# Self attention on one core: output casts moved to ScalarE, casts ahead of the exponentials, three waits for maxima dropped

## The chip, the cores and the metric

The kernel runs on one core of a Trainium2 chip. The metric is the device time of one execution, in microseconds (us): the median of the runs shown.

## What is computed

A transformer block on x of shape (4, 1024, 256): self attention, cross attention to a context of 77 rows, and a feed-forward part, each with a residual. The change is in the self attention alone. From the reference, cut to this:

```
attn_in = _adaln(x, cond, ln1_w, ln1_b, g1_w, g1_b, b1_w, b1_b)
x = _attn(attn_in, attn_in, sa_wq, sa_wkv, sa_wo, sa_bo) + x

def _attn(xq, ctx, wq, wkv, wo, bo):        # H, DH = 16, 64
    q = _heads(xq @ wq)
    k, v = jnp.split(ctx @ wkv, 2, axis=-1)
    k = _heads(k)
    v = _heads(v)
    q = _rope(q, sq, cq)
    k = _rope(k, sk, ck)
    sim = jnp.einsum('bhnd,bhmd->bhnm', q, k) * DH ** (-0.5)
    a = jax.nn.softmax(sim, axis=-1)
    o = jnp.einsum('bhnm,bhmd->bhnd', a, v)
    ...
    return o @ wo + bo
```

## The kernel before, in words

Each engine runs its own list of instructions in the order in which the code writes it; nothing else schedules them. Engines wait for each other through semaphores (`wait_ge`).

The self attention works through 32 head pairs (G = 4 batches x 8 pairs of heads; `g` in the code, numbered 0 to 31). A pair has eight **key tiles** of 128 keys (`kt`, 0 to 7). While pair g is being attended to, pair g+1's score maxima are estimated, pair g+2's keys and pair g+3's queries are projected and rotated, and pair g-1's output is divided by its sums and split. In one tile:

- TensorE: `differences` (L451), `scores` (L474), `bases` (L458), `shift` (L481), which subtracts the estimated maxima, then `values` of the tile before in two halves (L496). Between the two halves stands, by tile, a projection (L55: keys in tiles 0 and 1, queries in 4 and 5), the second half of the values' projection (L43, tile 2), a norm's transposes (L531), the sums (L506, tile 0) or the output product. At the end of tile 7 the maxima are transposed (L651) and the next pair's values projected (L43). Ahead of what stands between the halves TensorE waits for the first half of the tile's maxima (L621, `maxima_free(j, kt, 1)`), and ahead of the next tile's `differences` for the second half. All of these use the PSUM tile `ps_t`, which is why they take turns.
- ScalarE: `rises` (L692) reads what `differences` wrote, then two `exponentials` of 128x1024 (L704). By tile also: `high` (L688), which casts a rotated key or query to its f16 high part; `evacuate_kq` (L678), which takes a projected half out of PSUM, and for which the next `differences` waits; `evacuate_v` (L683), `evacuate_o` (L711), `evacuate_sums` (L717); `row` (L696), the negated maxima as a row. In pairs with a norm: `logarithms` (L721), `inverse_roots` (L726), `normalise` (L730), `norm_affine` (L737) and `norm_high` (L742).
- VectorE: `maxima` (L869) in two halves of 128x512, then `add_probs` (L882) twice. By tile also: `multiply` (L848, L849) and `rotated` (L853, and L856 for the key differences), `low` (L861), `reciprocals` (L886), `divide` (L892), and `split_output`: the cast of the divided output to its high half (L897) and the low half as the difference (L899). In pairs with a norm: statistics (L909, L915) and `norm_low` (L957).
- SyncE's queue carries the swaps of the rotation, the row of maxima, the gathering of sums and the broadcast of their inverses.

Pairs differ: 5, 10, 16, 21 and 28 take the statistics of the next norm, the two pairs that lie 2 and 3 behind these have its transposes in tiles 3 and 6, and pairs 9, 17 and 25 have the output product of a whole batch between their tiles.

## Time and profile before

| | us |
|---|---|
| median of 3 runs | 2208.25 |
| lowest, highest | 2205.37, 2210.38 |
| profiled execution | 2206.14 |
| its span | 2204.2 |

The profile is of one execution. "Busy" is the time in which an engine had an instruction in work; matmuls overlap, and their ends are modelled. In a timeline, rows are in order of start, a bracket at the end gives the idle time before the row and what ended it, and rows of a kind are merged (x4 are four instructions). The start of a pair or a tile is here the start of its first `differences` (L451). The self attention takes the time from about 75 to 1558 us; the cross attention and the feed-forward part follow.

### The profile page before, as it was taken

The numbers are of one execution on the slowest core, as the hardware profiler recorded it, in microseconds if no ns is written. First come the engines' busy times: TensorE is split into PE (matmuls) and PEld (weight loads), VectorE is DVE, ScalarE is ACT, GpSimd is POOL, SyncE is SP. The second block draws the span as 40 slices with busy tenths as digits, with TensorE's granted clock in tenths as the row PEclk, the third lists the DMA queues.
The fourth block names the chain that finished last, engine by engine and source line by source line (L and its number), as shares of the span: only waits on it lengthen the run. The fifth ranks groups of instructions, "written<-read, shape, count | busy, mean of one in ns | idle before, by whom it ended". The sixth has DMA issues, their size and how long they took to land. (4 is left out here: it accounts for less than half of the span.)

```text
span 2204.2 us, 40751 instructions
## 1 busy us (share of the span) xinstructions
PE 2057.2 (93%) x16360; PEld 919.9 (42%) x16360; DVE 1787.5 (81%) x2793; ACT 1395.5 (63%) x1774; POOL 9.0 (0%) x10
## 2 busy tenths in 40 slices
PE   4799999999999999999999999999988999986999
PEld 2233333336333334533333453333632444454676
DVE  6789899986998999699999869987688888845654
ACT  4577767774777777577777657776367666633442
POOL 1000000000000000000000000000000000000000
PEclk8799999999999999999999999999998999987999
DMA  6010110011110101011101112111232333324111
GB/s 191 37 39 31 49 49 37 33 49 49 49 50 30 59 30 50 30 68 49 39 30 45 35 46 72 40 49 40 79 120 93 108 122 123 122 77 120 39 39 39
DMA packets 99281, 135.42 MB, mean 61 GB/s; under 512 B 34501, under 2 KB 72343, under 8 KB 99095
## 3 DMA queue, kind: packets, MB, share of 16 engines
q1 hardware_dynamic: 99095, 132.83, 18.3%
q8 instruction: 130, 2.13, 0.4%
q14 instruction: 56, 0.46, 0.1%
HBM read 67.29 MB, written 13.11 MB: 36 GB/s over the span
## 5 line engine op out<-in xcount | busy, mean ns | idle before, releaser
L704 ACT ACTIVATE sa_probs<-sa_ps_s 128x1024 f32<-128x1024 f32 x512 | 496.6, 1022 | 212.5 <-PE sa_ps_s L481 212.4
L496 PE MATMUL sa_ps_o<-sa_probs,sa_v_pair 128*64 128x512 f32 x2048 | 534.7, 611 | 11.3 <-DVE sa_mx L869 11.3
L882 DVE TENSOR_TENSOR sa_acc<-sa_acc,sa_probs 128x1024 f32<-128x1024 f32 x384 | 452.9, 1221 | 18.7 <-ACT sa_probs L704 10.8
L869 DVE CUSTOM_DVE_ANT_0 sa_rise<-sa_ps_t,sa_rise 128x512 f32<-128x512 f32 x504 | 327.2, 687 | 132.1 <-PE sa_ps_t L458 130.5
L474 PE MATMUL sa_ps_s<-scores_or_weights 64*128 64x512 f16 x3072 | 376.3, 377 | 1.2 <-ACT raw_or_keys L678 1.2
L692 ACT ACTIVATE sa_rise<-sa_ps_t 128x1024 f32<-128x1024 f32 x252 | 257.6, 1022 | 151.5 <-PE sa_ps_t L451 150.4
L474 PEld LDWEIGHTS sa_ps_s<-scores_or_weights 64*128 64x128 f16 x3072 | 155.4, 94 | 153.6 <-ACT sa_v_pair L683 6.8
L496 PEld LDWEIGHTS sa_ps_o<-sa_probs,sa_v_pair 128*64 128x64 f32 x2048 | 113.7, 135 | 164.8 <-issue 97.0
L451 PE MATMUL sa_ps_t<-sa_kd,scores_or_weights 64*128 64x512 f16 x504 | 99.6, 389 | 37.1 <-ACT raw_or_keys L678 17.6
L451 PEld LDWEIGHTS sa_ps_t<-sa_kd,scores_or_weights 64*128 64x128 f16 x504 | 26.3, 93 | 220.7 <-issue 183.2
L458 PE MATMUL sa_ps_t<-scores_or_weights 64*128 64x512 f16 x504 | 98.8, 386 | 10.4 <-ACT sa_rise L692 10.4
L481 PE MATMUL sa_ps_s<-sa_m_line,sa_m_ones 32*128 32x512 f16 x1024 | 101.2, 385 | 0.0
L882 DVE TENSOR_TENSOR sa_acc<-sa_probs 128x1024 f32<-128x1024 f32 x64 | 75.6, 1222 | 8.4 <-ACT sa_probs L704 6.0
L848 DVE TENSOR_TENSOR raw_or_keys<-raw_or_keys,ropeC 128x1024 f32<-128x1024 f32 x64 | 78.1, 1220 | 4.6 <-DMA sa_swp<-raw_or_keys 4.5
L678 ACT ACTIVATE raw_or_keys<-sa_ps_t 128x512 f32<-128x512 f32 x118 | 70.9, 601 | 15.0 <-PE sa_ps_t L55 13.9
L43 PE MATMUL ca_ps_t<-xT_hi,scores_or_weights 128*128 128x512 f16 x256 | 79.3, 392 | 0.0
L861 DVE TENSOR_TENSOR scores_or_weights<-raw_or_keys,scores_or_weights 128x1024 f16<-128x1024 f32 x62 | 75.6, 1219 | 1.7 <-ACT scores_or_weights L688 1.7
L853 DVE TENSOR_TENSOR raw_or_keys<-raw_or_keys,sa_swp 128x1024 f32<-128x1024 f32 x62 | 75.8, 1222 | 1.1
L849 DVE TENSOR_TENSOR sa_swp<-sa_swp,ropeS 128x1024 f32<-128x1024 f32 x62 | 75.6, 1219 | 0.0
L1991 ACT ACTIVATE ff_hid<-ff_ps_h,ff_b_col 128x1024 f32<-128x1024 f32 x32 | 35.6, 1114 | 61.3 <-PE ff_ps_h L43 61.3
L43 PE MATMUL ca_ps_t<-scores_or_weights,ca_o_hi 128*128 128x256 f16 x400 | 74.2, 283 | 0.0
L43 PE MATMUL ff_ps_y<-w_hi,ff_h_hi 128*128 128x256 f16 x256 | 69.8, 273 | 3.5 <-DVE ff_h_lo L2090 3.5
(322 smaller groups left out, 3636.0 us busy)
## 6 DMA issues: line engine op xcount, KB each, us to landing
sa_swp<-raw_or_keys SPq DMA_DIRECT2D x124, 256.0 KB, 2.4
sa_inv<-sa_scratch SPq DMA_DIRECT2D x128, 128.0 KB, 3.0
ca_swp<-raw_or_keys SPq DMA_DIRECT2D x64, 256.0 KB, 2.3
ca_inv<-ca_scratch SPq DMA_DIRECT2D x64, 256.0 KB, 3.9
sa_xs<-in_x SPq DMA_DIRECT2D x4, 1024.0 KB, 5.8
sa_xr<-in_x SPq DMA_DIRECT2D x4, 1024.0 KB, 7.1
x_after_cross<-scores_or_weights SPq DMA_DIRECT2D x32, 128.0 KB, 2.0
ff_xr<-x_after_cross SPq DMA_DIRECT2D x4, 1024.0 KB, 5.7
```

The lines of the kernel that those rows point to most:

```text
L43: ins = pe.matmul(out, lhs[a][lhs_at(k)], rhs[b][rhs_at(k)], start=(start and i == 0), stop=(stop and i == len(terms) - 1))
L451: ins = pe.matmul(max_banks(j, t)[:, half(x)], hi[rows(x), j % 3, 1, t * P:(t + 1) * P], kd[rows(x), j % 2, :], start=True, stop=True)
L458: ins = pe.matmul(max_banks(j, t)[:, half(x)], hi[rows(x), j % 3, 1, t * P:(t + 1) * P], hi[rows(x), j % 3, 0, 0:HALF], start=True, stop=True)
L474: pe.matmul(ps_s[c][:, half(x)], k[rows(x), s, 0, ks], q[rows(x), s, 1, half(c)], start=(n == 0), stop=False)
L481: ins = pe.matmul(ps_s[c][:, half(x)], m_ones[quarter, :], m_line[quarter, :], start=False, stop=True)
L496: ins = pe.matmul(ps_o[rows(x), half(c)], v_pair[:, kt, rows(x)], probs[:, kt % 2, c, half(x)], start=(kt == 0), stop=(kt == NK - 1))
L692: act.activation(rise_of(j, t), max_banks(j, t), ACT.Relu).then_inc(s_rise, 1)
L704: act.activation(probs[:, kt % 2, c, :], ps_s[c][:, :], ACT.Exp, scale=float(DH) ** -0.5).then_inc(s_p, 1)
L848: dve.tensor_tensor(raw[:, i, :], raw[:, i, :], ropeC[:, :], ALU.mult).then_inc(s_mul[i], 1)
L853: dve.tensor_tensor(raw[:, i, :], raw[:, i, :], swapped(j, i)[:, :], ALU.add).then_inc(s_rot[i], 1)
L869: dve.tensor_tensor_reduce(out=larger, in0=max_banks(j, t)[:, half(x)], in1=larger, scale=1.0, scalar=-3.0e38, op0=ALU.add, op1=ALU.max, a ...
L882: dve.tensor_tensor(acc[:, c, :], before, probs[:, kt % 2, c, :], ALU.add).then_inc(s_acc[c], 1)
```

## The change

It has four parts.

1. On ScalarE `high(g+2, 1)` moves from behind tile 1's exponentials to ahead of them, and `high(g+2, 0)` from behind tile 5's exponentials to ahead of tile 6's.
2. The cast to the output's high half goes from VectorE to ScalarE: `split_output` becomes `high_output` (ScalarE, ahead of the exponentials of tile 5 for half 0 and of tile 7 for half 1; both in tile 7 in pairs 9, 17 and 25) and `low_output` (VectorE).
3. VectorE's order within a pair: `reciprocals` ahead of `low` in tile 1, `divide` of half 0 in tile 4 ahead of the rotation instead of tile 5, of half 1 in tile 5 instead of 6, and the key differences on their own in tile 5.
4. TensorE's wait for the first half of the maxima is dropped in tiles where nothing stands between the two halves of `values` (3, 6 and 7, unless a norm's transpose is there).

```diff
-                    if j < G:
+                    if j < G and (kt in K_AT + Q_AT + (V_SECOND,) or norm_bank(g, kt) is not None):
                         maxima_free(j, kt, 1)
...
+            def high_output(g, c):
+                act.wait_ge(s_div, 2 * g + c + 1)
+                if g >= PAIRS and g % PAIRS == 0:
+                    act.wait_ge(s_y, TT * (g // PAIRS))
+                act.activation(o_hi[:, g % PAIRS, half(c)], o_pair[:, half(c)], ACT.Copy).then_inc(s_ohi, 1)
...
+                    if kt == 1 and g + 2 < G:
+                        high(g + 2, 1)
+                    if kt == 5 and g >= 1 and not late_norm(g):
+                        high_output(g - 1, 0)
+                    if kt == 6 and g + 2 < G:
+                        high(g + 2, 0)
+                    if kt == 7 and g >= 1:
+                        if late_norm(g):
+                            high_output(g - 1, 0)
+                        high_output(g - 1, 1)
                     if g >= 0:
                         for c in order(kt):
                             exponentials(g, kt, c)
...
-                    if kt == 1 and g + 2 < G:
-                        high(g + 2, 1)
-                    if kt == 5 and g + 2 < G:
-                        high(g + 2, 0)
...
-            for n in range(2, len(following)):
+            for n in range(2, 5):
+                following_high(n)
+            for c in range(2):
+                high_output(G - 1, c)
+            for n in range(5, len(following)):
                 following_high(n)
...
-                if i == 0:
-                    dve.wait_ge(s_rot[0], j + 1)
-                    dve.tensor_tensor(kd[:, j % 2, :], raw[:, 0, HALF:N], raw[:, 0, 0:HALF],
-                                      ALU.subtract).then_inc(s_kd, 1)
+
+            def key_differences(j):
+                dve.wait_ge(s_rot[0], j + 1)
+                dve.tensor_tensor(kd[:, j % 2, :], raw[:, 0, HALF:N], raw[:, 0, 0:HALF],
+                                  ALU.subtract).then_inc(s_kd, 1)
...
-            def split_output(g, c):
+            def low_output(g, c):
                 n, cs = 2 * g + c + 1, half(c)
-                dve.wait_ge(s_div, n)
-                dve.tensor_copy(o_hi[:, g % PAIRS, cs], o_pair[:, cs]).then_inc(s_ohi, 1)
                 dve.wait_ge(s_ohi, n)
                 dve.tensor_tensor(o_lo[:, g % PAIRS, cs], o_pair[:, cs], o_hi[:, g % PAIRS, cs],
                                   ALU.subtract).then_inc(s_ot, 1)
...
+                    if kt == 1 and g >= 1:
+                        reciprocals(g - 1)
                     if kt == 1 and g + 2 < G:
                         low(g + 2, 1)
-                    if kt == 1 and g >= 1:
-                        reciprocals(g - 1)
                     if kt == 2 and g + 2 < G:
                         multiply(g + 2, 0)
+                    if kt == 4 and g >= 1:
+                        divide(g - 1, 0)
                     if kt == 4 and g + 2 < G:
                         rotated(g + 2, 0)
...
+                    if kt == 5 and g + 2 < G:
+                        key_differences(g + 2)
+                    if kt == 5 and g >= 1 and not late_norm(g):
+                        low_output(g - 1, 0)
                     if kt == 5 and g >= 1:
-                        divide(g - 1, 0)
-                        if not late_norm(g):
-                            split_output(g - 1, 0)
-                    if kt == 6 and g >= 1:
                         divide(g - 1, 1)
-                    if kt == 6 and late_norm(g) and g + 2 < G:
-                        low(g + 2, 0)
...
-                    if kt == 7 and g + 2 < G and not late_norm(g):
+                    if kt == 7 and g + 2 < G:
                         low(g + 2, 0)
                     if kt == 7 and g >= 1:
                         if late_norm(g):
-                            split_output(g - 1, 0)
-                        split_output(g - 1, 1)
+                            low_output(g - 1, 0)
+                        low_output(g - 1, 1)
```

How it stands in the engines' lists is shown at three places of pair 15; the changed file has other line numbers, given in the words. First ScalarE in tile 1 and the start of tile 2, before (L692 is a rise, L704 the exponentials, L688 the cast of the query, L678 the evacuation of a projected key):

```order
L692 ACTIVATE sa_rise<-sa_ps_t 128x1024
L704 ACTIVATE sa_probs<-sa_ps_s 128x1024 x2
L688 ACTIVATE scores_or_weights<-raw_or_keys 128x1024
L678 ACTIVATE raw_or_keys<-sa_ps_t 128x512
L692 ACTIVATE sa_rise<-sa_ps_t 128x1024
```

and the same place after:

```order
L692 ACTIVATE sa_rise<-sa_ps_t 128x1024
L688 ACTIVATE scores_or_weights<-raw_or_keys 128x1024
L704 ACTIVATE sa_probs<-sa_ps_s 128x1024 x2
L678 ACTIVATE raw_or_keys<-sa_ps_t 128x512
L692 ACTIVATE sa_rise<-sa_ps_t 128x1024
```

The cast has passed the two exponentials and stands right behind the rise. Next ScalarE in tiles 5 and 6, before:

```order
L692 ACTIVATE sa_rise<-sa_ps_t 128x1024
L704 ACTIVATE sa_probs<-sa_ps_s 128x1024 x2
L688 ACTIVATE scores_or_weights<-raw_or_keys 128x1024
L678 ACTIVATE raw_or_keys<-sa_ps_t 128x512
L692 ACTIVATE sa_rise<-sa_ps_t 128x1024
L704 ACTIVATE sa_probs<-sa_ps_s 128x1024 x2
```

and after (L717 is now `high_output`):

```order
L692 ACTIVATE sa_rise<-sa_ps_t 128x1024
L717 ACTIVATE sa_o_hi<-sa_o_pair 128x512
L704 ACTIVATE sa_probs<-sa_ps_s 128x1024 x2
L678 ACTIVATE raw_or_keys<-sa_ps_t 128x512
L692 ACTIVATE sa_rise<-sa_ps_t 128x1024
L688 ACTIVATE scores_or_weights<-raw_or_keys 128x1024
L704 ACTIVATE sa_probs<-sa_ps_s 128x1024 x2
```

The cast of the key has left the place between exponentials and evacuation in tile 5 for tile 6, and the output cast has come into tile 5. Last VectorE from tile 4's sums (L882) to the first maxima of tile 6 (L869), before:

```order
L882 TENSOR_TENSOR sa_acc<-sa_acc,sa_probs 128x1024 x2
L853 TENSOR_TENSOR raw_or_keys<-raw_or_keys,sa_swp 128x1024
L856 TENSOR_TENSOR sa_kd<-raw_or_keys 128x512
L869 ISA sa_rise,sa_mx<-sa_ps_t,sa_rise 128x512
L869 ISA sa_mx 128x1
L869 ISA sa_rise,sa_mx<-sa_ps_t,sa_rise 128x512
L869 ISA sa_mx 128x1
L882 TENSOR_TENSOR sa_acc<-sa_acc,sa_probs 128x1024 x2
L892 TENSOR_TENSOR sa_o_pair<-sa_o_pair,sa_inv 128x512
L897 CAST sa_o_hi<-sa_o_pair 128x512
L899 TENSOR_TENSOR sa_o_lo<-sa_o_pair,sa_o_hi 128x512
L869 ISA sa_rise,sa_mx<-sa_ps_t,sa_rise 128x512
```

and after (L899 now are the sums, L909 the divide, L869 the rotation, L886 the maxima, L873 the key differences, L914 the low half):

```order
L899 TENSOR_TENSOR sa_acc<-sa_acc,sa_probs 128x1024 x2
L909 TENSOR_TENSOR sa_o_pair<-sa_o_pair,sa_inv 128x512
L869 TENSOR_TENSOR raw_or_keys<-raw_or_keys,sa_swp 128x1024
L886 ISA sa_rise,sa_mx<-sa_ps_t,sa_rise 128x512
L886 ISA sa_mx 128x1
L886 ISA sa_rise,sa_mx<-sa_ps_t,sa_rise 128x512
L886 ISA sa_mx 128x1
L899 TENSOR_TENSOR sa_acc<-sa_acc,sa_probs 128x1024 x2
L873 TENSOR_TENSOR sa_kd<-raw_or_keys 128x512
L914 TENSOR_TENSOR sa_o_lo<-sa_o_pair,sa_o_hi 128x512
L909 TENSOR_TENSOR sa_o_pair<-sa_o_pair,sa_inv 128x512
L886 ISA sa_rise,sa_mx<-sa_ps_t,sa_rise 128x512
```

The divide of half 0 now stands ahead of the rotation, the key differences behind tile 5's sums, and the cast is gone.

## Rows read from the trace of the kernel before

**Rows 1.** The page, part 1: busy time, share and instructions of each engine.

```profile
PE 2057.2 (93%) x16360; PEld 919.9 (42%) x16360; DVE 1787.5 (81%) x2793; ACT 1395.5 (63%) x1774; POOL 9.0 (0%) x10
```

**Rows 2.** Windows of pairs 15, 14, 10: length, busy per engine, TensorE's clock, DMA.

```profile
772.21:815.18 42.97, 42.16 (x331) 15.88 (x331) 39.77 (x63) 30.60 (x36) 0.00 (x0) 1.00 0.11 38
728.86:772.21 43.35, 42.35 (x332) 15.79 (x331) 40.30 (x64) 30.69 (x36) 0.00 (x0) 1.00 0.20 62
...
549.42:594.51 45.09, 43.00 (x332) 15.49 (x331) 42.23 (x81) 33.34 (x40) 0.00 (x0) 1.00 0.19 60
```

**Rows 3.** TensorE's waits, 120 to 1560 us: for whom; total, times, longest.

```profile
PE sa_ps_t L451 <- ACT raw_or_keys L678: 14.6, 36, 0.4
PE sa_ps_o L496 <- DVE sa_mx L869: 8.6, 13, 2.1
PE sa_ps_t L55 <- DVE sa_mx L869: 7.0, 25, 0.5
```

**Rows 4.** Timeline of TensorE, pair 14, ends of tiles 1 and 4: start, length.

```profile
740.40 1.03 PE L496 MATMUL sa_ps_o<-sa_probs,sa_v_pair 128*64 128x512 f32 x4
741.83 0.39 PE L451 MATMUL sa_ps_t<-sa_kd,scores_or_weights 64*128 64x512 f16 x2 [0.41 <-ACT raw_or_keys L678]
...
755.85 1.03 PE L496 MATMUL sa_ps_o<-sa_probs,sa_v_pair 128*64 128x512 f32 x4
756.81 0.39 PE L451 MATMUL sa_ps_t<-sa_kd,scores_or_weights 64*128 64x512 f16 x2
```

**Rows 5.** Timeline of ScalarE, pair 14, tile 1 and the end of tile 4.

```profile
736.47 1.02 ACT L692 ACTIVATE sa_rise<-sa_ps_t 128x1024 f32<-128x1024 f32 x1
738.32 1.94 ACT L704 ACTIVATE sa_probs<-sa_ps_s 128x1024 f32<-128x1024 f32 x2 [0.82 <-PE sa_ps_s L481]
740.14 1.06 ACT L688 ACTIVATE scores_or_weights<-raw_or_keys 128x1024 f16<-128x1024 f32 x1
741.09 0.60 ACT L678 ACTIVATE raw_or_keys<-sa_ps_t 128x512 f32<-128x512 f32 x1
...
756.05 0.60 ACT L678 ACTIVATE raw_or_keys<-sa_ps_t 128x512 f32<-128x512 f32 x1 [0.35 <-PE sa_ps_t L55]
```

**Rows 6.** Timeline of VectorE, pair 14, tile 0 and the start of tile 6.

```profile
728.89 0.68 DVE L957 TENSOR_TENSOR xT_lo<-sa_xn,xT_hi 128x512 f16<-128x512 f32 x1
...
731.70 0.68 DVE L869 CUSTOM_DVE_ANT_0 sa_rise<-sa_ps_t,sa_rise 128x512 f32<-128x512 f32 x1
...
732.91 1.22 DVE L848 TENSOR_TENSOR raw_or_keys<-raw_or_keys,ropeC 128x1024 f32<-128x1024 f32 x1
734.05 1.22 DVE L849 TENSOR_TENSOR sa_swp<-sa_swp,ropeS 128x1024 f32<-128x1024 f32 x1
735.30 1.22 DVE L853 TENSOR_TENSOR raw_or_keys<-raw_or_keys,sa_swp 128x1024 f32<-128x1024 f32 x1
...
763.17 0.43 DVE L897 CAST sa_o_hi<-sa_o_pair 128x512 f16<-128x512 f32 x1
763.63 0.69 DVE L899 TENSOR_TENSOR sa_o_lo<-sa_o_pair,sa_o_hi 128x512 f16<-128x512 f32 x1
```

**Rows 7.** Timeline of ScalarE, pair 10's tile 7 and pair 12's tile 6.

```profile
590.40 1.28 ACT L704 ACT_TABLE_LOAD   x1
...
593.62 0.25 ACT L696 ACTIVATE sa_m_rows<-sa_ps_t 16x128 f16<-16x128 f32 x1
...
677.80 0.63 ACT L742 ACTIVATE xT_hi<-sa_xn 128x512 f16<-128x512 f32 x1
678.34 1.02 ACT L692 ACTIVATE sa_rise<-sa_ps_t 128x1024 f32<-128x1024 f32 x1
```

**Rows 8.** Timelines of pair 31: VectorE in tile 4, ScalarE and TensorE around tile 5.

```profile
1543.07 2.36 DVE L882 TENSOR_TENSOR sa_acc<-sa_acc,sa_probs 128x1024 f32<-128x1024 f32 x2 [1.97 <-ACT sa_probs L704]
...
1545.61 1.94 ACT L704 ACTIVATE sa_probs<-sa_ps_s 128x1024 f32<-128x1024 f32 x2 [1.66 <-PE sa_ps_s L481]
...
1547.36 1.47 PE L474 MATMUL sa_ps_s<-scores_or_weights 64*128 64x512 f16 x12
```

More of the change, by code:

```diff
@@ L1040, in _ @@
                 rotated(0, i)
+                if i == 0:
+                    key_differences(0)
             weights_low(4)
@@ L1048, in _ @@
                 rotated(1, i)
+                if i == 0:
+                    key_differences(1)
             for n in range(2):
@@ L1118, in _ @@
                 divide(G - 1, c)
-                split_output(G - 1, c)
+                low_output(G - 1, c)
             dve.wait_ge(s_x, 16 * B)
```

## The prediction

> **What bounds the kernel now.** The views were read in this order: the page's busy shares, the windows of single head pairs, TensorE's waits, and then the timelines of the three engines around each wait. The page gives TensorE 2057.2 us of 2204.2 us, VectorE 1787.5, ScalarE 1395.5 [rows 1]. The change touches only the self attention, which runs 32 head pairs of eight key tiles (0 to 7) from about 75 to 1558 us. A pair with no extra work (pair 15) takes 42.97 us, and TensorE is busy for 42.16 of them, VectorE for 39.77, ScalarE for 30.60 [rows 2]. The granted clock there is 1.00. So TensorE bounds, and only its own waits can be won. They are short and of few kinds [rows 3]: 14.6 us in 36 waits for ScalarE's evacuation of a projected key or query (L678), 7.0 us in 25 and 8.6 us in 13 for VectorE's maxima (L869) ahead of L55 and L496. That is 30.2 us in all, 1.4% of the time, and hardly more can be won here; further waits, for the norm's evacuation and for rises, the change leaves as they are.
>
> The recorded idle time is slightly less than a wait costs. After the last value products of tile 1 (L496 at 740.40) the next tile's L451 starts at 741.83, 1.43 us later; after those of tile 4 (755.85) it starts at 756.81, 0.96 us later and without a wait [rows 4]. So such a wait costs **0.47 us**, where the trace calls 0.41 idle.
>
> The Trainium skill ("Perfetto Trace Analysis", Identifying the Most-Contended Engine) says that matmul busy time is no measure of TensorE's distance from its limit, and that the share of weight loads is: here 42%. By that TensorE would have room and another engine would set the pace, which is the rival "no gain" below; the tiles that run without any wait speak against it.
>
> **The change, part by part.**
>
> *1. The cast of a rotated query (high(g+2, 1), L688) goes ahead of tile 1's exponentials.* Now ScalarE runs rise, 0.82 us idle, two exponentials, L688 at 740.14, and L678 at 741.09, 0.95 us later; the last one frees TensorE [rows 5]. In tile 4, where nothing stands between, L678 starts 0.20 us after L496's start (756.05 against 755.85), once its projection is done, and nobody waits [rows 4, 5]. Moved, L688 fills the 0.82 us gap: rise starts at 736.47, the next ScalarE instruction can follow 0.95 us later (its own pace at L688 to L678), so L688 runs from 737.42 and the exponentials from 738.37 instead of 738.32. Its input is ready: the rotation (L853 at 735.30, 1.22 us [rows 6]) ends at 736.52. The wait goes, worth 0.47 us. It occurs in 27 pairs (0 to 29 without 9, 17, 25). Pair 0 has weight casts in the same place and its rotation is late there: nothing. Five pairs (5, 10, 16, 21, 28) hold the next norm's statistics on VectorE (part 5): nothing. 21 x 0.47 = **9.9 us**.
>
> *2. The cast of a rotated key (high(g+2, 0)) goes from behind tile 5's exponentials to ahead of tile 6's.* The same wait stands at the start of tile 6 in the ten pairs 1, 4, 6, 11, 14, 15, 20, 22, 26, 27. In its place in tile 5 comes the new output cast (L717, high_output), again in the 0.82 us gap. 10 x 0.47 = **4.7 us**. Tile 6 is the shortest, about 4 us: rise, L688 and two exponentials are 0.95 + 0.95 + 1.83 = 3.73 us, so it fits.
>
> *3. VectorE's part.* It loses 64 casts at a pace of 0.46 us (763.17 to 763.63) [rows 6], and the same 64 appear on ScalarE, where a cast of just this shape paces at 0.54 us (677.80 to 678.34) [rows 7]. Where a piece of the norm (norm_low, L957 at 728.89) is still queued at the start of a pair, VectorE reaches tile 0's maxima only at 731.70 and L55 waits [rows 6]; that makes pair 14 0.38 us longer than pair 15 (43.35 against 42.97) [rows 2]. With the cast gone the maxima come 0.46 us earlier, and the wait goes. It is in ten pairs (3, 4, 8, 9, 13, 14, 19, 20, 24, 25): **3.8 us**. In tile 5 the order divide, rotate replaces rotate, key differences. An instruction of 128x1024 is followed after 1.14 us (732.91 to 734.05), but after 1.25 us by one that needs its result (734.05 to 735.30) [rows 6], as the differences need the rotation's; the new order saves this 0.1 us. It counts where VectorE is late in tile 5, in ten pairs with norm transposes: **1.0 us**.
>
> *4. The wait for the first half of the maxima (s_max) in tiles 3, 6 and 7.* In ordinary pairs nobody waits there; worth nothing. Five pairs wait 0.42 us in tile 3 and 0.52 us in tile 6 (they are among L496's 13 waits [rows 3]), but next L451 needs the second half of the same maxima anyway.
>
> *5. The five pairs with statistics (45.09 us, VectorE 42.23 [rows 2]).* From tile 1 to 6 VectorE runs there without a pause, so TensorE's earlier start only meets the next maxima. In tile 6 and 7 ScalarE is tight: rise, table load (590.40, 1.28 us), exponentials behind it (591.68), and the row of maxima at 593.62, which the next pair needs [rows 7]. The output cast now stands ahead of that load and moves all this by 0.54 us. The next pair starts at 594.51, and needs the row (0.25 us long) by then: 593.62 + 0.54 + 0.25 = 594.41, just in time; the value projection (L43) waits some 0.2 us. 5 x 0.2 = **1.0 us lost**.
>
> *6. Rest.* Ten tiles 6 with norm transposes start their evacuation (L737) 0.05 us later: **0.5 us lost**. In pair 31 there are no rises to cover, and high_output(30, 0) must wait for a divide behind tile 4's sums, which now end at 1545.4; plus 0.61 and 0.54 this gives exponentials at 1546.6 instead of 1545.61 [rows 8]. TensorE has 1.75 us until tile 6 (1547.36), so some 0.3 to 0.5 us are lost, and 0.46 us come back at the end, where the last cast left VectorE: **0.2 us lost** at most. In the tail TensorE multiplies until after the divides; nothing.
>
> **Sum:** 9.9 + 4.7 + 3.8 + 1.0 - 1.0 - 0.5 - 0.2 = 17.7 us. The trace is of an execution of 2206.14 us (span 2204.2, 1.9 around it), 2.1 below the median of 2208.25; a shortening applies to both: 2188.4 there and **2190.6** as a median. Bounds: the unseen operation is L717; nearest rows are VectorE's own cast (0.46) and L742 (0.54), both inside the 0.82 us gap, and I take L742's, the same engine and shape. The price of a wait lies between 0.41 and 0.47: 31 waits make 1.9 us between the ends. If parts 5 and 6 cost double, 1.7 us more.
>
> **Rivals.**
> *A. The order crosses engines too often.* Divide on VectorE, cast on ScalarE, subtract on VectorE replaces a chain on one engine. If ScalarE is held by the late divide, or each cast costs its 0.54 - 0.46 = 0.08 us more on the path, 64 x 0.08 = 5.1 us and part 2's 4.7 us go: gain 7.9 us, 2200.3. For it: tile 6 leaves only 0.3 us on ScalarE. Against: the divide of tile 4 should end about 0.9 us into tile 5, rise ends at 1.45. The Trainium skill ("ScalarE: Activation LUTs", Rules for kernel authors) puts elementwise arithmetic on VectorE, as the faster engine; this trace agrees on a cast (0.43 against 0.63 us long), and by that rule this rival is the outcome.
>
> *B. No gain.* VectorE, 39.8 of 43 us busy, follows TensorE so closely that each won 0.47 us returns as a wait for maxima. For it: it happens in part 5. Against: in pair 15 it has 3.2 us of slack, and it is given 0.9 us by the casts. Only part 3's 3.8 us would be left: 2204.4.
>
> *C. Slower.* ScalarE is in order, and high_output(g-1, 0) now stands ahead of tile 5's exponentials. If the divide ends after the rise, the exponentials, the query's evacuation and the next L451 all wait. The first 0.37 us are covered (0.35 idle before L678 in a free tile [rows 5]), and 0.47 are part 2's own gain; so it gets worse than now once the divide ends over 0.84 us after rise's end, 1.4 us later than I count. At 2 us late in 29 pairs: 29 x (2 - 0.37) = 47 us lost, against 13 won otherwise: 2242. The divide also needs the broadcast inverses, but nothing on VectorE waits for them now before the tail.
>
> *D. More.* The removed waits pay in the five pairs after all: 5 x (0.47 + 0.42 + 0.52) = 7 us: 2183.6.
>
> **How the numbers follow.** Forecast (2186 to 2196) 0.62; A (2196 to 2203.8) 0.17; D 0.07; B 0.10; C 0.04. A change of under 0.2% (4.4 us) can't be told from none. Faster by more than that: 0.62 + 0.17 + 0.07 = 0.86; within: B's 0.10; slower: 0.04. The range 2183.5 to 2201 leaves B, C and the far ends of A and D out.
>
> **What would show it.** Pair 15 should take 42.0 us (42.97 - 0.94), pair 14 42.0, pairs with statistics 45.1 to 45.3. TensorE's waits for L678 should be gone but for pair 0, those of L55 for maxima reduced to about 15 in tile 5. ScalarE's exponentials in tiles 1, 5, 6 should start within 0.1 us of now, relative to the tile. An exponential held by the divide in tile 5 would show C or A; new waits of L55 or L451 for L886's maxima in plain pairs would show B.

## The result, and the profile after

| | before | changed |
|---|---|---|
| median, us | 2206.81 (4 runs) | 2185.50 (4 runs) |
| lowest, highest | 2200.60, 2210.38 | 2181.04, 2186.95 |
| profiled execution, its span | 2206.14, 2204.2 | 2181.04, 2179.3 |

The changed kernel is faster: the ratio is 0.9903, with a 95% interval of 0.9882 to 0.9924. The median is 21.3 us lower; 17.7 had been forecast.

From the start of pair 0 to the first output product of the last batch (L515) the two profiles take 1483.56 and 1460.86 us: **22.7 us less**. The rest of the difference of spans (24.9) lies outside the change: the changed kernel's pair 0 started 0.9 us later, and what follows that L515 took 642.4 instead of 645.5 us. Further on, profiles with the same code there show 639.3 to 649.0 us for it, so whole times scatter by some microseconds, while a single head pair from 1 to 29 repeats to 0.02 us. Pair 0 and the last two pairs don't repeat: pair 0 took 51.75 us here and 53.14 in a later run whose code differs from this one's in later pairs only. What is firm is the 23.3 us won in pairs 1 to 29; pair 0 won 0.6 more and the last two lost 1.2, and neither repeats. The readings below go by pairs and tiles.

Windows of pairs 15, 14 and 10 of the changed kernel, in this order, with the columns of [rows 2]:

```profile
760.69:802.72 42.03, 42.03 (x332) 15.80 (x331) 38.90 (x61) 31.61 (x38) 0.00 (x0) 1.00 0.11 39
718.67:760.69 42.02, 42.02 (x331) 15.79 (x330) 39.39 (x62) 31.61 (x38) 0.00 (x0) 1.00 0.20 64
542.23:587.04 44.81, 42.90 (x331) 15.47 (x330) 41.57 (x79) 34.24 (x42) 0.00 (x0) 1.00 0.18 60
```

In pairs 15 and 14 TensorE is now busy from end to end. Against [rows 2] they are 0.94 and 1.33 us shorter, as forecast; pair 10, for which 45.1 to 45.3 us had been expected, is not longer but 0.28 shorter.

TensorE's waits from 120 to 1540 us, as in [rows 3]; VectorE's maxima are now L886, the norm's evacuation L743:

```profile
PE sa_ps_t L458 <- ACT sa_rise L692: 8.2, 14, 1.0
PE sa_ps_t L451 <- ACT sa_xn L743: 4.5, 22, 0.2
PE sa_ps_t L451 <- DVE sa_mx L886: 3.5, 11, 0.8
PE sa_ps_o L496 <- DVE sa_mx L886: 3.4, 2, 2.7
PE sa_ps_t L55 <- DVE sa_mx L886: 3.3, 10, 0.4
```

The 36 waits for L678 are gone. Those of L55 fell from 25 to 10 named ones, in tiles 4 and 5 of the five statistics pairs (ten more of 0.14 us in tile 5 have no releaser named). Ahead of L451 there are new waits for the maxima, in tiles 4 and 7 of the statistics pairs and in tile 7 of pair 29: they are the dropped waits, come back one instruction later. With the wait kept, in a run below, all of them are gone.

The end of tile 1 in pair 14, TensorE and then ScalarE, to be held against [rows 4] and [rows 5]:

```profile
729.83 1.03 PE L496 MATMUL sa_ps_o<-sa_probs,sa_v_pair 128*64 128x512 f32 x4
730.79 0.39 PE L451 MATMUL sa_ps_t<-sa_kd,scores_or_weights 64*128 64x512 f16 x2
```

```profile
725.90 1.02 ACT L692 ACTIVATE sa_rise<-sa_ps_t 128x1024 f32<-128x1024 f32 x1
726.81 1.06 ACT L688 ACTIVATE scores_or_weights<-raw_or_keys 128x1024 f16<-128x1024 f32 x1
727.75 1.94 ACT L704 ACTIVATE sa_probs<-sa_ps_s 128x1024 f32<-128x1024 f32 x2
730.04 0.60 ACT L678 ACTIVATE raw_or_keys<-sa_ps_t 128x512 f32<-128x512 f32 x1 [0.34 <-PE sa_ps_t L55]
```

L451 follows the value products after 0.96 us instead of 1.43. The cast fills the gap behind the rise: the exponentials start 1.85 us after the rise, as before (738.32 - 736.47), and the evacuation waits for TensorE (0.34 us) instead of the other way round. In tile 5 the same gap takes the output cast, 0.62 us long, and 0.31 us of it stay idle:

```profile
746.20 1.02 ACT L692 ACTIVATE sa_rise<-sa_ps_t 128x1024 f32<-128x1024 f32 x1 [0.59 <-PE sa_ps_t L451]
747.12 0.62 ACT L717 ACTIVATE sa_o_hi<-sa_o_pair 128x512 f16<-128x512 f32 x1
748.05 1.94 ACT L704 ACTIVATE sa_probs<-sa_ps_s 128x1024 f32<-128x1024 f32 x2 [0.31 <-PE sa_ps_s L481]
```

And VectorE at the start of pair 14 [rows 6]: without the cast the maxima start 2.37 us into the pair instead of 2.84.

```profile
718.70 0.69 DVE L972 TENSOR_TENSOR xT_lo<-sa_xn,xT_hi 128x512 f16<-128x512 f32 x1
719.30 1.22 DVE L878 TENSOR_TENSOR scores_or_weights<-raw_or_keys,scores_or_weights 128x1024 f16<-128x1024 f32 x1
720.44 0.69 DVE L914 TENSOR_TENSOR sa_o_lo<-sa_o_pair,sa_o_hi 128x512 f16<-128x512 f32 x1
721.04 0.69 DVE L886 CUSTOM_DVE_ANT_0 sa_rise<-sa_ps_t,sa_rise 128x512 f32<-128x512 f32 x1
```

### The profile page after: what moved, and what is told of

Read it like the earlier page. It is cut to its first block and busy times, and to the rows that moved or that the text cites. A ratio compares the mean times of both kernels' runs of the same rounds, so it can differ in the third digit from the quotient of the medians.

```text
span 2179.3 us, 40686 instructions
## 1 busy us (share of the span) xinstructions
PE 2050.5 (94%) x16360; PEld 918.1 (42%) x16360; DVE 1754.6 (81%) x2729; ACT 1425.6 (65%) x1838; POOL 9.0 (0%) x10
## 5 line engine op out<-in xcount | busy, mean ns | idle before, releaser
L704 ACT ACTIVATE sa_probs<-sa_ps_s 128x1024 f32<-128x1024 f32 x512 | 496.0, 1021 | 133.3 <-PE sa_ps_s L481 133.2
L496 PE MATMUL sa_ps_o<-sa_probs,sa_v_pair 128*64 128x512 f32 x2048 | 532.0, 610 | 3.4 <-DVE sa_mx L886 3.4
L899 DVE TENSOR_TENSOR sa_acc<-sa_acc,sa_probs 128x1024 f32<-128x1024 f32 x384 | 453.1, 1222 | 22.3 <-ACT sa_probs L704 15.1
L886 DVE CUSTOM_DVE_ANT_0 sa_rise<-sa_ps_t,sa_rise 128x512 f32<-128x512 f32 x504 | 327.4, 688 | 141.6 <-PE sa_ps_t L458 140.8
L692 ACT ACTIVATE sa_rise<-sa_ps_t 128x1024 f32<-128x1024 f32 x252 | 257.4, 1022 | 152.7 <-PE sa_ps_t L451 151.4
L496 PEld LDWEIGHTS sa_ps_o<-sa_probs,sa_v_pair 128*64 128x64 f32 x2048 | 115.8, 135 | 151.8 <-issue 126.7
L451 PE MATMUL sa_ps_t<-sa_kd,scores_or_weights 64*128 64x512 f16 x504 | 99.8, 391 | 28.4 <-DVE sa_mx L886 9.0
L451 PEld LDWEIGHTS sa_ps_t<-sa_kd,scores_or_weights 64*128 64x128 f16 x504 | 25.1, 93 | 211.7 <-issue 167.5
L678 ACT ACTIVATE raw_or_keys<-sa_ps_t 128x512 f32<-128x512 f32 x118 | 70.9, 601 | 40.0 <-PE sa_ps_t L55 40.0
L899 DVE TENSOR_TENSOR sa_acc<-sa_probs 128x1024 f32<-128x1024 f32 x64 | 75.6, 1222 | 10.0 <-ACT sa_probs L704 7.2
L869 DVE TENSOR_TENSOR raw_or_keys<-raw_or_keys,sa_swp 128x1024 f32<-128x1024 f32 x62 | 75.8, 1223 | 1.1
```

The source lines that it names most:

```text
L451: ins = pe.matmul(max_banks(j, t)[:, half(x)], hi[rows(x), j % 3, 1, t * P:(t + 1) * P], kd[rows(x), j % 2, :], start=True, stop=True)
L496: ins = pe.matmul(ps_o[rows(x), half(c)], v_pair[:, kt, rows(x)], probs[:, kt % 2, c, half(x)], start=(kt == 0), stop=(kt == NK - 1))
L692: act.activation(rise_of(j, t), max_banks(j, t), ACT.Relu).then_inc(s_rise, 1)
L704: act.activation(probs[:, kt % 2, c, :], ps_s[c][:, :], ACT.Exp, scale=float(DH) ** -0.5).then_inc(s_p, 1)
L869: dve.tensor_tensor(raw[:, i, :], raw[:, i, :], swapped(j, i)[:, :], ALU.add).then_inc(s_rot[i], 1)
L886: dve.tensor_tensor_reduce(out=larger, in0=max_banks(j, t)[:, half(x)], in1=larger, scale=1.0, scalar=-3.0e38, op0=ALU.add, op1=ALU.max, a ...
```

## The experiments

The theory is that of the prediction: TensorE sets the time, and each part of the change takes away its own short waits, so that the parts add up. Rivals were named for each run. Differences of tiles and pairs are between the starts of tiles in two profiles; "pairs 0 to 29" is from the start of pair 0 to the start of pair 30.

### Part 1 alone: the query and key casts ahead of the exponentials

```diff
+                    if kt == 1 and g + 2 < G:
+                        high(g + 2, 1)
+                    if kt == 6 and g + 2 < G:
+                        high(g + 2, 0)
                     if g >= 0:
                         for c in order(kt):
                             exponentials(g, kt, c)
...
-                    if kt == 1 and g + 2 < G:
-                        high(g + 2, 1)
-                    if kt == 5 and g + 2 < G:
-                        high(g + 2, 0)
```

> Before with part 1 alone: the two casts of rotated keys and queries ahead of the exponentials. Theory (parts add up): the wait of 0.47 us goes at the end of tile 1 in 26 pairs and of tile 5 in the 10 plain ones, so pair 15 takes 42.0 us, pair 14 42.4 (its tile 0 wait stays), and the kernel is 12.2 + 4.7 = 17 us shorter, less some 1 us where a statistics pair gives the start back. Rival (VectorE becomes the bound without the cast taken off it): pair 15 stays above 42.5 us and the gain is under 10 us.

Measured: ratio 0.9926 (0.9898 to 0.9953), median 2191.18 against 2208.84. Pairs 0 to 29 are 17.16 us shorter. Pairs 15, 14 and 10:

```profile
763.40:805.43 42.03, 42.03 (x331) 15.67 (x330) 39.61 (x63) 30.58 (x36) 0.00 (x0) 1.00 0.11 39
721.00:763.40 42.40, 42.21 (x331) 15.57 (x329) 40.13 (x64) 30.69 (x36) 0.00 (x0) 1.00 0.20 63
543.88:588.58 44.70, 42.92 (x331) 15.40 (x331) 42.05 (x81) 33.21 (x40) 0.00 (x0) 1.00 0.18 61
```

Pair 15 reaches the same 42.03 us as in the changed kernel, with all of VectorE's casts still in place, so VectorE doesn't bound a plain pair. Pair 10 wins 0.47 us in tile 1 and gives back only 0.07 in tile 3: that is where the prediction had counted nothing.

### Parts 2 and 3 alone: the output cast on ScalarE, and VectorE's order

The changed kernel with the two other parts undone:

```diff
-                    if j < G and (kt in K_AT + Q_AT + (V_SECOND,) or norm_bank(g, kt) is not None):
+                    if j < G:
                         maxima_free(j, kt, 1)
...
-                    if kt == 1 and g + 2 < G:
-                        high(g + 2, 1)
...
-                    if kt == 6 and g + 2 < G:
-                        high(g + 2, 0)
...
+                    if kt == 1 and g + 2 < G:
+                        high(g + 2, 1)
+                    if kt == 5 and g + 2 < G:
+                        high(g + 2, 0)
                     if kt in K_AT and g + 2 < G:
```

> The changed kernel without the moved query and key casts and with the wait for maxima: only the output cast on ScalarE and VectorE's order. Theory: tile 0 waits gone (4.7 us in all), tiles 1 and 5 as before, pair 15 at 42.97 us, statistics pairs 0.2 us longer in tile 7, pair 30 1.5 us longer in tile 5: 2 to 4 us faster than before. Rival (the output cast ahead of tile 5's exponentials delays the evacuation further): tile 5 longer than before in plain pairs, no gain.

Measured: ratio 0.9971 (0.9955 to 0.9987). Pairs 0 to 29 are 4.5 us shorter, pairs 30 and 31 together 1.2 us longer, net 3.3, inside the 2 to 4 expected. (The clock fell there behind tile 5's pause, as in the changed kernel; see the last section.) Pairs 15, 14 and 10:

```profile
769.59:812.55 42.96, 42.16 (x331) 15.89 (x329) 39.03 (x61) 31.62 (x38) 0.00 (x0) 1.00 0.12 38
726.62:769.59 42.97, 42.16 (x332) 15.89 (x331) 39.55 (x62) 31.62 (x38) 0.00 (x0) 1.00 0.19 62
547.65:592.86 45.21, 43.18 (x332) 15.40 (x331) 41.76 (x79) 34.33 (x42) 0.00 (x0) 1.00 0.18 60
```

Pair 14 loses its 0.38 us of tile 0, pair 15 is unchanged: two casts more on ScalarE cost a plain pair nothing. Pair 10 is 0.12 us longer, with +0.21 us in tile 7.

### Part 4 alone: the wait for the maxima dropped

```diff
-                    if j < G:
+                    if j < G and (kt in K_AT + Q_AT + (V_SECOND,) or norm_bank(g, kt) is not None):
                         maxima_free(j, kt, 1)
```

> Before with the dropped wait for maxima alone. Theory: nothing in plain pairs; statistics pairs shorten tile 3 by about 0.3 us and give it back in tile 4, since VectorE sets the time; 0.09 us twice in pairs 9, 17, 25; in all within 1 us of before. Rival (the removed waits pay): 5 x 0.9 = 4.7 us faster.

Measured: ratio 0.9977 (0.996 to 0.9995), pairs 0 to 29 shorter by 1.77 us, and from pair 0 to L515 by 0.6. In the five statistics pairs tiles 3, 4, 6 and 7 change by -0.40, +0.40, -0.40 and +0.39: nothing won. 0.09 us come in tiles 3 and 6 of pairs 9, 17 and 25, 0.4 in pair 29, 0.6 in pair 0, which doesn't repeat. Pairs 30 and 31 are 1.2 us longer: 0.4 is pair 29's, given back in tile 0 of pair 30, and 0.8 come in tiles 5 and 6, where the clock fell. The median is 6.7 us lower, and the interval of the ratio leaves out 1; the self attention of the profile explains 0.6 of it, and I take the rest for scatter outside it, but have not shown that.

The parts alone give 17.16 + 4.50 + 1.77 = 23.4 us in pairs 0 to 29, the changed kernel 23.9; without pair 0, 22.5 and 23.3. They add up in all tiles but one. Tile 5 of the ten pairs with transposes is 0.14 us shorter in the changed kernel, 1.4 us in all, and 0.01 to 0.03 us with parts 1 or 3 alone. With the output cast and VectorE's order alone, L55 starts there 3.38 us into the tile instead of 3.50 (pair 13), but the evacuation stands behind the cast L688 and starts at 5.05 us as before; with both it starts at 4.90. So this gain belongs to the two parts together.

### The changed kernel with the wait kept

```diff
-                    if j < G and (kt in K_AT + Q_AT + (V_SECOND,) or norm_bank(g, kt) is not None):
+                    if j < G:
```

> The changed kernel with the wait for the first half of the maxima kept in tiles 3, 6 and 7 (part 4 of the change undone). Theory: VectorE and ScalarE set the time where this wait is, so a statistics pair's tile 6 is 0.4 us longer and its tile 7 0.4 shorter; plain pairs are the same, pairs 9, 17 and 25 0.2 us longer: under 1 us slower than the changed kernel. Rival (the waits pay once the casts are moved): 3 us slower.

Measured: ratio 0.9902 (0.9885 to 0.9918), beside 0.9876 (0.9862 to 0.9891) for the changed kernel on the same chip. By tiles the difference is small: pairs 0 to 29 are 0.72 us longer than in the changed kernel's second profile, statistics pairs +0.40, -0.40, +0.40, -0.40 in tiles 3, 4, 6 and 7, pairs 9, 17, 25 +0.19 each. The rival (3 us) falls here by the profiles. The medians (2185.49 against 2179.36) are further apart than the self attention explains; I take that for the scatter of whole times, but have not shown it.

### The changed kernel again

> The changed kernel itself once more, beside before on one chip, to see how far whole times scatter and how far single pairs repeat. Theory: every pair from 1 to 29 takes the same time as in the first profile within 0.05 us; the median is 20 to 25 us under before, since the self attention alone is 22.7 us shorter. Rival (part of the gain is in what follows the self attention): the self attention's shortening and the median's differ by more than 4 us again.

Measured: median 2179.36 against 2207.87, ratio 0.9876 (0.9862 to 0.9891). All pairs from 1 to 29 are within 0.02 us of the first profile, those of 64 us included. Pairs 15, 14 and 10:

```profile
760.40:802.44 42.04, 42.04 (x331) 15.78 (x329) 38.88 (x61) 31.64 (x38) 0.00 (x0) 1.00 0.11 39
718.38:760.40 42.02, 42.02 (x331) 15.76 (x329) 39.38 (x62) 31.63 (x38) 0.00 (x0) 1.00 0.20 64
541.92:586.73 44.81, 42.92 (x331) 15.46 (x330) 41.56 (x79) 34.27 (x42) 0.00 (x0) 1.00 0.18 60
```

The median's shortening (28.5 us) is again not the self attention's (21.4 in this profile, where pair 30 takes 1.2 us more); the medians of the same two kernels were 21.3 us apart the first time and 28.5 this time. The expected 20 to 25 was missed by the median, and the rival's sign, more than 4 us between the two shortenings, appeared (7.1). That part of the gain lies behind the self attention is still not shown: from L515 on the profiles take 643.1 to 648.5 us with the code of before there and 639.3 to 649.0 with the changed one. A difference of a microsecond or two there can't be told from this scatter.

### The output cast back on VectorE

The changed kernel, `high_output` taken out of ScalarE's list and done in `low_output`:

```diff
             def low_output(g, c):
                 n, cs = 2 * g + c + 1, half(c)
+                dve.wait_ge(s_div, n)
+                dve.tensor_copy(o_hi[:, g % PAIRS, cs], o_pair[:, cs]).then_inc(s_ohi, 1)
                 dve.wait_ge(s_ohi, n)
```

> The changed kernel with the output's cast back on VectorE, right ahead of the subtraction; all else as changed. Theory: the tile 0 waits come back (0.38 us in 10 pairs, 0.17 in 5), and tile 5 of pairs with transposes loses nothing; statistics pairs win 0.23 us each in tile 7, since nothing stands ahead of the second table load. Sum: 3.8 + 0.9 - 1.2 = 3.5 us slower than the changed kernel. Rival (the cast on ScalarE costs on the path): as fast as the changed kernel or faster.

Measured: ratio 0.9941 (0.9921 to 0.9961); pairs 0 to 29 are 7.0 us longer than in the changed kernel, twice the 3.5 expected. What was expected is there: 0.38 us in tile 0 of ten pairs, and a net gain of 0.23 in the end of a statistics pair (+0.47 in tile 6, -0.70 in tile 7). Three places had been missed. Pair 26, a plain pair behind one with an output product:

```profile
764.02:806.04 42.02, 42.02 (x331) 15.77 (x329) 39.53 (x63) 30.58 (x36) 0.00 (x0) 1.00 0.11 39
1290.02:1332.88 42.86, 42.21 (x331) 15.67 (x329) 40.55 (x65) 30.68 (x36) 0.00 (x0) 1.00 0.27 87
```

Pair 15 (first row) loses nothing, pair 26 (second row) 0.8 us, all in tile 0. So do pairs 10 and 18. At the end of pairs 9, 17 and 25 VectorE has the low part of the key and both halves of the output to do behind tile 7's sums, since the change moved `low` there from tile 6, and with two casts more it reaches the next pair's first maxima 0.82 us later. Before, with the casts but with `low` in tile 6, these pairs lost nothing; nor do they in the changed kernel, with `low` in tile 7 but without the casts. The other two places are tile 6 of pair 29 (0.46 us), where TensorE waits for the maxima anyway and VectorE now has a cast more ahead of them, and tile 6 of the ten pairs with transposes (0.06 us each). So the cast's move and the new order belong together.

### The divide left until tile 5

The changed kernel, with the divide between tile 5's maxima and its sums. It prices the rival that ended slower: ScalarE's cast, and the exponentials behind it, then wait for the divide.

```diff
+                    if kt == 5 and g >= 1:
+                        divide(g - 1, 0)
                     if g >= 0 and kt >= 1:
                         for c in range(2):
                             add_probs(g, kt, c)
...
-                    if kt == 4 and g >= 1:
-                        divide(g - 1, 0)
```

> The changed kernel with the divide of half 0 between tile 5's maxima and its sums instead of in tile 4, so that ScalarE's output cast, and the exponentials behind it, wait for it. This prices rival C of the prediction. Theory: the divide ends 3.8 us into tile 5, the exponentials start at 4.4 instead of 2.28; 0.4 to 0.5 us are covered by the idle time ahead of the evacuation, the rest stands: tile 5 is some 1.7 us longer in the 25 pairs that evacuate a query there (1 to 28 without 9, 17, 25), in all about 42 us slower than the changed kernel, 2227 us. Rival (TensorE has other work to cover it): under 20 us slower.

Measured: median 2223.47, ratio to before 1.0073 (1.0046 to 1.0101): slower than before, and pairs 0 to 29 are 38.9 us longer than in the changed kernel. ScalarE in tile 5 of pair 15 (the tile starts at 806.16):

```profile
806.59 1.03 ACT L692 ACTIVATE sa_rise<-sa_ps_t 128x1024 f32<-128x1024 f32 x1 [0.58 <-PE sa_ps_t L451]
810.05 0.63 ACT L717 ACTIVATE sa_o_hi<-sa_o_pair 128x512 f16<-128x512 f32 x1 [2.44 <-DVE sa_o_pair L909]
810.59 1.92 ACT L704 ACTIVATE sa_probs<-sa_ps_s 128x1024 f32<-128x1024 f32 x2
812.40 0.60 ACT L678 ACTIVATE raw_or_keys<-sa_ps_t 128x512 f32<-128x512 f32 x1
```

The exponentials start 4.43 us into the tile, and L451 of tile 6 waits until 813.14: the tile takes 6.98 us instead of 5.32. Of the 2.15 us of delay 0.49 are covered and 1.66 stand, in plain pairs and in those right behind statistics, and 1.40 in the others. The mechanism of the prediction's rival C is right, and its price nearly (it had 0.37 us covered); the pairs it counted are 29, and 25 evacuate a query in tile 5. So 37.6 us were lost in these, and 38.9 with pairs 29 and 0, and not 29 x (2.15 - 0.37) = 52. In pairs 1 to 28 of the changed kernel it doesn't occur, since the divide ends 0.98 us into tile 5. In pairs 29 and 30 it does: the cast waits 0.71 and 0.85 us for the divide, and the exponentials start 2.84 us into tile 5, 0.4 and 0.6 later than before. No query is projected there, so nothing stands behind it.

### The cast behind the table load in statistics pairs

```diff
                     if kt == 7 and g >= 1:
                         if late_norm(g):
                             high_output(g - 1, 0)
-                        high_output(g - 1, 1)
+                        if norm_of(g, 0) is None:
+                            high_output(g - 1, 1)
...
                         row(j)
+                        if g >= 1 and norm_of(g, 0) is not None:
+                            high_output(g - 1, 1)
                         evacuate_v(j, 0)
```

> The changed kernel; in the five pairs with statistics the cast of half 1 goes from ahead of tile 7's table load to behind the row of maxima. Theory: tile 7 gives back the 0.2 us that the cast costs there, 1 us in all in five pairs, nothing elsewhere. Rival (the loss of tile 7 is only what earlier tiles won, given back by VectorE): no difference.

Measured: ratio 0.9886 (0.9862 to 0.9911). Tile 7 of all five pairs is 0.23 us shorter, 1.2 us in all, and tile 0 of the five pairs behind them 0.09; no other tile of pairs 1 to 29 moves, and together they are 1.5 us shorter. Pair 0, in which nothing was changed, took 1.4 us more. In the changed kernel ScalarE does this in pair 10, tile 7:

```profile
581.68 1.00 ACT L692 ACTIVATE sa_rise<-sa_ps_t 128x1024 f32<-128x1024 f32 x1
582.59 0.62 ACT L717 ACTIVATE sa_o_hi<-sa_o_pair 128x512 f16<-128x512 f32 x1
583.22 1.28 ACT L704 ACT_TABLE_LOAD   x1
584.52 1.94 ACT L704 ACTIVATE sa_probs<-sa_ps_s 128x1024 f32<-128x1024 f32 x2
```

This is the one place in which the gap of 0.82 us behind the rise didn't exist, since the table load had filled it [rows 7].

### All idle waits, and a combined version

```diff
-                    if j < G and (kt in K_AT + Q_AT + (V_SECOND,) or norm_bank(g, kt) is not None):
+                    if j < G and ((kt in K_AT and g + 2 < G) or (kt in Q_AT and g + 3 < G) or kt == V_SECOND or
+                                  norm_bank(g, kt) is not None):
                         maxima_free(j, kt, 1)
```

> The changed kernel with the wait for the first half of the maxima dropped also where pairs 29 and 30 project nothing (tiles 4 and 5, in pair 30 tiles 0 and 1 too). Theory: TensorE still waits for the second half ahead of the next tile, so only 0.3 us are won per tile; if the pause in pair 30's tile 5 gets below 2.45 us, the clock stays at full and 0.9 us more are won. 0.5 to 2 us faster. Rival: the pause is as long as before, the clock falls, no gain.

Measured: ratio 0.9873 (0.9847 to 0.99). Pair 29 gives 0.40 us back in tile 6 as everywhere; pair 30's tile 5 is 1.3 us shorter, and with tile 6 pairs 30 and 31 are 1.4 us shorter. TensorE still pauses 2.47 us there, and the clock stayed at full. The gain isn't the edit's: the run above, without this edit and with its clock at full there too, takes 80.84 us for pairs 30 and 31, this one 80.79. At the same clock the edit wins 0.4 us in tile 5 and loses it in tile 6. Nor did the expectation's 2.45 us decide over the clock: it fell behind shorter pauses and stayed behind a longer one (last section).

The combined version has these two edits and two more:

```diff
-                    if norm_of(g, 2) is not None and kt == 0:
+                    if norm_of(g, 2) is not None and kt == 1:
                         normalise(norm_of(g, 2), TT - 1)
...
-                    if g == G - 2 and kt in (2, 4):
-                        n = kt // 2 - 1
+                    if (g, kt) in ((G - 2, 2), (G - 1, 2)):
+                        n = g - (G - 2)
                         following_rest(n)
                         following_low(n)
```

> The two edits before together, and two more: the last of the eight normalisations two pairs behind the statistics moves from tile 0 to tile 1, behind the evacuation (it holds up tile 1's rise by 0.48 us in five pairs, and in pair 30), and the second low half of the following weights moves from pair 30's tile 4 to pair 31's tile 2, where VectorE idles. Theory: 1.0 + 2.9 + 1.5 (the pause in pair 30's tile 5 and the clock's fall go) and the 0.5 of before: 5 to 6 us faster than the changed kernel, 2180 us. Rival (the moved normalisation delays tile 2's rise): 3 us at most.

Measured: median 2174.15 against 2208.87, ratio 0.9846 (0.9819 to 0.9874), the fastest of all. From pair 0 to L515 it takes 1452.95 us, 7.9 less than the changed kernel's first profile, where 5 to 6 had been expected. 4.1 us come in pairs 0 to 29 and 3.8 in pairs 30 and 31; of these 1.4 are the clock, which stayed at full. Pairs 15, 12 and 10:

```profile
758.58:800.60 42.02, 42.02 (x331) 15.77 (x330) 38.88 (x61) 31.64 (x38) 0.00 (x0) 1.00 0.12 39
627.78:672.16 44.38, 43.84 (x340) 16.54 (x339) 39.36 (x62) 34.54 (x43) 0.00 (x0) 1.00 0.11 37
540.90:585.48 44.58, 42.74 (x333) 15.48 (x331) 41.85 (x79) 34.26 (x42) 0.00 (x0) 1.00 0.19 61
```

Pair 12 was 44.86 us in the changed kernel: the moved normalisation wins 0.48 in each of five pairs. Pair 30's tile 5 takes 4.15 instead of 7.86 us. A plain pair stays at 42.02, with TensorE busy throughout: there nothing is left to win by waits.

## Why the prediction was right, and where it was off

The main steps held: TensorE bounds, its waits for L678 went, and what they cost came back whole. The number forecast was 17.7 us; the self attention won 22.7, and the medians differ by 21.3. By tiles, with what the prediction had for each (a minus is time lost):

| step | predicted, us | measured, us |
|---|---|---|
| tile 1's wait for L678 | 21 x 0.47 = 9.9 | 26 x 0.47 = 12.2 |
| tile 5's wait for L678 | 10 x 0.47 = 4.7 | 4.7 |
| tile 0's wait for maxima | 3.8 | 4.7 |
| tile 5 of pairs with transposes | 1.0 | 1.4 |
| statistics pairs, tiles 3 to 7 | -1.0 | -0.9 |
| tile 6 with transposes | -0.5 | 0.0 |
| pairs 9, 17, 25, tiles 3 and 6 | 0 | 0.5 |
| pair 29's tiles 5 to 7 | 0 | 0.6 |
| pair 0 (doesn't repeat) | 0 | 0.6 |
| pairs 30 and 31 (the clock fell) | -0.2 | -1.2 |
| sum | 17.7 | 22.6 |

- **The price of a wait** is 0.47 us, where the trace marks 0.41 idle. The step of comparing two tiles' distances, in place of adding up idle times, was right to 0.01 us. The prediction used it only where a row marks a wait, and so missed tile 0 of pairs 6, 11, 17, 22 and 29, which held 0.18 us of waiting each that no row marks (0.9 us).
- **The gap of 0.82 us** took in each cast in tiles 1, 5 and 6, and the exponentials stayed within 0.02 us of where they were, but for tile 5 of pairs 29 and 30. L717 measures 0.62 us, against the 0.63 of the row taken for it.
- **Mis-sized: "from tile 1 to 6 VectorE runs there without a pause"** (part 5). This is 2.3 of the 4.9 us. VectorE had some slack in tile 2 of statistics pairs, in pieces too short for the trace to mark. Before, from the start of tile 1's sums to the first maxima of tile 2, and from these to the sums:

```profile
559.55 2.36 DVE L882 TENSOR_TENSOR sa_acc<-sa_probs 128x1024 f32<-128x1024 f32 x2
...
563.95 0.69 DVE L869 CUSTOM_DVE_ANT_0 sa_rise<-sa_ps_t,sa_rise 128x512 f32<-128x512 f32 x1
...
565.35 2.36 DVE L882 TENSOR_TENSOR sa_acc<-sa_acc,sa_probs 128x1024 f32<-128x1024 f32 x2
```

  That is 4.40 and 1.40 us. The changed kernel does the same instructions in 4.18 and 1.21:

```profile
552.39 2.36 DVE L899 TENSOR_TENSOR sa_acc<-sa_probs 128x1024 f32<-128x1024 f32 x2
...
556.57 0.68 DVE L886 CUSTOM_DVE_ANT_0 sa_rise<-sa_ps_t,sa_rise 128x512 f32<-128x512 f32 x1
...
557.78 2.36 DVE L899 TENSOR_TENSOR sa_acc<-sa_acc,sa_probs 128x1024 f32<-128x1024 f32 x2
```

  0.41 us of slack took up most of the 0.47 that TensorE came earlier. The run with part 1 alone shows it in another way: 0.07 given back, no more. That the forecast came out 4.9 us under the 22.6 is mostly this step.
- **The cast ahead of the table load** cost 0.23 us a pair (0.2 forecast), shown by the run that moved it behind.
- **Tile 5 of pairs with transposes**: 0.14 us each, 0.1 forecast, but not by VectorE's order alone, as the prediction had it. The order brings L55 0.12 us earlier; without part 1 the evacuation then waits for L688, and the tile is no shorter.
- **Tile 6 with transposes**: the 0.05 us never came through; the norm's evacuation starts 4.11 us into the tile of pair 13 before and 4.10 after.
- **Pair 30** was not costed apart, and took 1.1 us more. The divide moved into tile 4, ahead of the low half of the following weights, and pushed the first maxima of tile 5 by 0.6 us; TensorE, which still waited for them, paused 2.72 instead of 2.11 us, and came back at a lower clock. The 0.6 us cost nothing: in the run with the cast behind the table load, with the same code, the same pause and a full clock, tile 5 takes 6.96 us instead of 6.37 before, tile 6 5.30 instead of 5.89, and pairs 30 and 31 take 80.84 us instead of 80.99. So the 1.2 us of the table are the clock. That the change made it fall is not shown: it also fell in two runs that left the divide where it was, behind 2.12 us (last section). In pair 31 the exponentials of tile 5 start at 1524.69, 4.58 us behind tile 4's, against 3.60 before, as the prediction worked out; 0.1 us of it is left at L515.
- **The tail** lost nothing: from L515 to the first instruction of the cross attention on VectorE it is 26.37 us before and 26.36 after.
- **The rivals.** A (the chain across engines costs) fell: a plain pair with all casts on ScalarE takes as long as one without. B (no gain) fell with it. C was priced and is real, but its condition is met only in pairs 29 to 31, and only pair 31 loses by it (0.3 us in tile 5, of which 0.1 are left in the end). D was right only in that the statistics pairs gained, 0.3 us each instead of 1.4, through slack, and not through the dropped waits.

## What to carry to other kernels

A wait of the bounding engine can be priced by holding the distance between the same two instructions against a tile without the wait; the idle time that a trace marks leaves out what is spread over overlapping instructions. An engine that is in order and idles between two steps of a chain has room for an independent instruction there, but its input must be ready: a cast put into that gap was free, and the same cast with an input 2.4 us late cost more than the whole change had won. Dropping a wait won next to nothing where the next instruction needs the next value of the same semaphore; look first at what ends second. And before a microsecond is put down to an edit, look at the granted clock of the stretch: here it fell or stayed with the same code.

## What the runs showed of the hardware

TensorE's clock fell to half after a pause in some runs and not in others, with the same pause in the same place. In pair 30, tile 5, TensorE waits 2.72 us for the maxima and then does four value products (L496). The granted clock (the third number from the end) of the changed kernel behind that pause, and then that of the kernel with the cast behind the table load, whose code is the same in this pair:

```profile
1487.00:1489.00 2.00, 1.97 (x6) 0.36 (x8) 2.00 (x4) 0.00 (x0) 0.00 (x0) 0.52 0.00 0
```

```profile
1486.00:1488.00 2.00, 2.00 (x14) 0.64 (x16) 2.00 (x4) 0.61 (x1) 0.00 (x0) 1.00 0.01 4
```

0.52 is near the lower of its two levels (1.2 of 2.4 GHz). The products themselves, in the same two kernels:

```profile
1487.03 1.98 PE L496 MATMUL sa_ps_o<-sa_probs,sa_v_pair 128*64 128x512 f32 x4 [2.72 <-DVE sa_mx L886]
```

```profile
1485.94 1.08 PE L496 MATMUL sa_ps_o<-sa_probs,sa_v_pair 128*64 128x512 f32 x4 [2.72 <-DVE sa_mx L889]
```

That cost 0.9 us in these products, and 1.4 by the end of the self attention. In the second profile of the changed kernel the lower clock lasted longer behind the same pause, and cost 2.5. The shorter pause of the old order is no protection. Before, and then the run with part 1 alone, the same place:

```profile
1509.71 1.08 PE L496 MATMUL sa_ps_o<-sa_probs,sa_v_pair 128*64 128x512 f32 x4 [2.11 <-DVE sa_mx L869]
```

```profile
1492.55 1.98 PE L496 MATMUL sa_ps_o<-sa_probs,sa_v_pair 128*64 128x512 f32 x4 [2.12 <-DVE sa_mx L869]
```

The run with part 4 alone shows the same behind 2.12 us (products of 1.58 us, then a granted clock of 0.50). Over all profiles the clock fell behind five of the six pauses of 2.72 us at this place, and behind two of the four of 2.11 or 2.12; too few to say whether the longer pause makes it likelier. In pair 0 a pause of 2.45 us was followed by the lower clock in the changed kernel; one of 2.47 us in pair 30 of the run with all idle waits dropped was not. So a pause of two microseconds or more on TensorE had a price of its own in some executions, on top of its length. What decides it was not tried.

The Trainium skill ("ScalarE: Activation LUTs", Rules for kernel authors) gives max, add, mul and the like to VectorE and not to ScalarE, as the engine that is faster per element. It names no cast; for one, this trace agrees in the length (0.43 us on VectorE against 0.62 on ScalarE), but the kernel with the output casts on VectorE was 7 us slower in pairs 0 to 29, since ScalarE had the room there and VectorE hadn't.
